# A mixture-of-experts stage on one core: routing and experts in one pass over batches of tiles

## What is computed

```python
def _L1_ffn_ref(x, router_w, router_b, expert_w, expert_b):
    router_probs = jax.nn.softmax(x @ router_w + router_b, axis=-1)
    top_p, top_i = jax.lax.top_k(router_probs, K)              # K = 2 of 8 experts
    top_p = top_p / jnp.sum(top_p, axis=-1, keepdims=True)
    expert_out = jnp.einsum('bnd,edc->bnec', x, expert_w) + expert_b
    gathered = jnp.take_along_axis(expert_out, top_i[..., None], axis=2)
    return jnp.einsum('bnk,bnkc->bnc', top_p, gathered)
...
t = t + _L1_ffn_ref(_ln_t(t), ...)                             # _ln_t: (t - mean) / sqrt(var + eps)
```

## Time and profile before

| | |
|---|---|
| median of three runs | 2795.91 us (2795.01 to 2797.33) |
| profiled execution | 2797.76 us |
| its span in the profile | 2795.8 us |
| TensorE busy | 2291.9 us, 82% |
| VectorE | 2198.8 us, 79% |
| ScalarE | 1640.6 us, 59% |
| GpSimd | 578.9 us, 21% |
| TensorE's granted clock, mean | 0.87 |

### The profile page before, as it was taken

One profiled execution on the slowest core, in us unless ns is written; L12 is line 12 of the kernel. 1 busy time (PEld: TensorE's weight loads), 2 busy tenths in 40 slices (PEclk: granted clock), 3 DMA queues, 4 the chain that ended last, 5 costly groups with the idle time before them and its releaser, 6 DMA issues. The chain is left out here.

```text
span 2795.8 us, 34597 instructions
## 1 busy us (share of the span) xinstructions
PE 2291.9 (82%) x10800; PEld 1298.5 (46%) x10800; DVE 2198.8 (79%) x3516; ACT 1640.6 (59%) x2225; POOL 578.9 (21%) x468
## 2 busy tenths in 40 slices
PE   0684646759760699999999999999999999768887
PEld 0681213747630344444444444444444444654554
DVE  5327889756598778888888888888888888668998
ACT  0113012632227478888888888888888888213665
POOL 0002340002106401210122012210200000004888
PEclk9996866555565799999999999999999999559999
DMA  4600212000004000000000000000000000000111
GB/s 148 222 19 1 120 44 78 0 9 1 1 1 121 5 1 1 1 1 1 1 1 1 1 1 1 1 1 1 1 1 1 1 1 1 9 0 16 34 34 38
DMA packets 81398, 63.93 MB, mean 23 GB/s; under 512 B 11745, under 2 KB 79329, under 8 KB 79729
## 3 DMA queue, kind: packets, MB, share of 16 engines
q1 hardware_dynamic: 74000, 60.28, 6.7%
q10 hardware_dynamic: 7264, 1.94, 0.3%
HBM read 36.97 MB, written 25.17 MB: 22 GB/s over the span
## 5 line engine op out<-in xcount | busy, mean ns | idle before, releaser
L1753 ACT ACTIVATE inner<-banks,key_bias,scales 128x1024 f32<-128x1024 f32 x512 | 617.3, 1206 | 211.0 <-PE banks L1626 205.8
L1875 DVE TENSOR_TENSOR weights_low<-weights,weights_high 128x1024 f16<-128x1024 f32 x512 | 675.5, 1319 | 17.1
L1760 ACT ACTIVATE weights<-inner 128x1024 f32<-128x1024 f32 x512 | 541.1, 1057 | 16.1 <-DVE weights_low L1875 0.3
L1871 DVE CAST weights_high<-weights 128x1024 f16<-128x1024 f32 x512 | 371.1, 725 | 180.7 <-ACT weights L1760 168.1
L1626 PE MATMUL banks<-queries_high,keys_high 128*128 128x512 f16 x1024 | 304.6, 379 | 0.7 <-ACT inner L1753 0.7
L1641 PE MATMUL banks<-weights_high,tokens_low 128*128 128x512 f16 x1024 | 304.6, 379 | 0.0
L1626 PE MATMUL banks<-queries_low,keys_high 128*128 128x512 f16 x1024 | 304.6, 379 | 0.0
L1641 PE MATMUL banks<-weights_low,tokens_high 128*128 128x512 f16 x1024 | 304.6, 379 | 0.0
L1626 PE MATMUL banks<-queries_high,keys_low 128*128 128x512 f16 x1024 | 304.6, 379 | 0.0
L1641 PE MATMUL banks<-weights_high,tokens_high 128*128 128x512 f16 x1024 | 304.5, 379 | 0.0
L1949 POOL CAST sums_high<-sums 128x512 f16<-128x512 f32 x32 | 39.4, 1230 | 1089.8 <-ACT sums L1743 1071.8
(11 more groups left out here) (432 smaller groups left out, 3751.3 us busy)
## 6 DMA issues: line engine op xcount, KB each, us to landing
images_a<-in_x SPq DMA_DIRECT2D x4, 2048.0 KB, 16.6
tokens_scratch<-images_a SPq DMA_DIRECT2D x4, 2048.0 KB, 13.1
images_b<-tokens_scratch SPq DMA_DIRECT2D x32, 256.0 KB, 2.8
mixed_scratch<-images_a SPq DMA_DIRECT2D x4, 2048.0 KB, 13.1
spare<-in_x SPq DMA_DIRECT2D x32, 256.0 KB, 2.9
result<-group_result SPq DMA_DIRECT2D x32, 256.0 KB, 2.3
images_b<-mixed_scratch SPq DMA_DIRECT2D x10, 768.0 KB, 5.3
table<-tables ACTq DMA_DIRECT2D x1, 805.5 KB, 14.3
```

What stands on the lines that cost most here:

```text
L1753: act.activation(m.inner[:, t % 2, :], m.pair[t % 2], ACT.Exp, scale=m.fs[:, 1:2], bias=m.kb[:, c // QN % 2, k:k + 1]).then_inc(s.inner, 1)
L1760: act.activation(m.wt[:, t % 2, :], m.inner[:, t % 2, :], ACT.Exp).then_inc(s.outer, 1)
L1871: vec.tensor_copy(m.wH[:, t % DEEP, :], m.wt[:, t % 2, :]).then_inc(s.high, 1)
L1875: vec.tensor_tensor(m.wL[:, t % DEEP, :], m.wt[:, t % 2, :], m.wH[:, t % DEEP, :], ALU.subtract)\
```

## The change

The two stages become one, `stage_ffn`.

- The token vectors are reflected so that the direction of all ones falls on the last coordinate. A centred vector has zero there. That row of the transposed tokens is set to 1.0 (`m.ln[..., D - 1:D]`, once), and the same row of the weights holds the biases. The weights are multiplied by the reflection (`m.house`) on TensorE at the start. Reflecting a token costs a changed mean (`TILT`); normalising is then `scale * x + bias` on ScalarE.
- Router weights are eight more columns beside the experts'. Logits are made by three `F32R` matmuls of 8 columns for each tile, from the same high and low parts as the experts'.
- The work is one pass over batches of 4, 8, 8, 8 and 4 groups. While the experts of one batch run, the next batch is normalised, turned, split and routed (`prep`, in a batch's first tiles), and its ranks and gates come in seven pieces in the batch's last eight tiles (`pieces`, `exps`). Sixteen groups fit in the ring of high and low parts (`RING`).
- VectorE adds experts 0 to 3 to the image by one multiply-add each, `u = bank * gate + acc`. The order is (n, 0), (n-1, 2), (n, 1), (n-1, 3), so that no multiply-add stands right behind the one it needs. GpSimd adds the four scaled by ScalarE (256, then 128 elements), and then `u`, in three instructions per tile.
- Banks 2, 3 and 7 hold VectorE's halves, 4 and 5 ScalarE's, 0 and 1 the transposes, 6 the logits. The expert matmuls of a tile are the same six. The loops are unrolled in full.

```diff
-            lambda: stage_router(nc, held, m, ins),
-            lambda: stage_experts(nc, held, m, out),
+            lambda: stage_ffn(nc, held, m, ins, out),
...
+BATCHES = [4, 8, 8, 8, 4]
+RING = 16
+SETTLE = 11
+def batch_plan():
+    first = [sum(BATCHES[:k]) for k in range(len(BATCHES))]
+    prep, pieces, exps = {}, {}, {}
+    for k in range(1, len(BATCHES)):
+        at, slots = first[k - 1] * GRP, BATCHES[k - 1] * GRP
+        for i in range(BATCHES[k]):
+            prep.setdefault(at + i * (slots - SETTLE) // BATCHES[k], []).append(first[k] + i)
+        for i in range(7):
+            pieces[at + slots - 8 + i] = k
+        exps[at + slots - 6] = k
...
+            def expert(n):
+                t, j = divmod(n, GRP)
+                pe.wait_ge(s.low, t + 1)
+                for h, bank in ((0, m.ps[DBANK[n % 3]]), (1, m.ps[ABANK[n % 2]])):
+                    if h == 0 and n >= 3:
+                        pe.wait_ge(s.chain, place[n - 3, 3] + 1)
+                    if h == 1 and n >= 2:
+                        pe.wait_ge(s.scaled, n - 1)
...
+            pe.wait_ge(s.loaded, 32)
+            for i in range(2):
+                pe.matmul(m.pair[1][:, 512 * i:512 * i + 512], m.house, m.w8[:, 512 * i:512 * i + 512], start=True, stop=True)
+            pe.matmul(m.pair[2][:, 0:EXPERTS], m.house, m.w8[:, EXPERTS * D:], start=True, stop=True).then_inc(s.weights, 1)
+            for t in range(BATCHES[0]):
+                turn(t)
+                if t >= 1:
+                    logit(t - 1)
+            logit(BATCHES[0] - 1)
+            for n in range(NI):
+                expert(n)
+                for t in prep.get(n - 2, []):
+                    logit(t)
+                for t in prep.get(n, []):
+                    turn(t)
...
+                    e = act.activation(m.ln[:, t % 2, j, 0:D - 1], m.b[:, img, 0:D - 1], ACT.Identity,
+                                       scale=m.fac[:, 1, img:img + 1], bias=m.fac[:, 2, img:img + 1])
...
+            for n in range(NI):
+                for t in prep.get(n, []):
+                    normed(t)
+                scaled(n)
+                for t in prep.get(n - 1, []):
+                    high(t)
+                if n in exps:
+                    exps_of(exps[n])
...
+                vec.scalar_tensor_tensor(out=m.u[:, n % 4, :], in0=m.ps[DBANK[n % 3]][:, e * D:e * D + D],
+                                         scalar=m.gate[:, n, e:e + 1], in1=acc, op0=ALU.mult, op1=ALU.add)\
+                    .then_inc(s.chain, 1)
...
+                add(n, 0)
+                add(n - 1, 2)
+                add(n, 1)
+                add(n - 1, 3)
+                for t in prep.get(n - 1, []):
+                    low(t)
...
+                    pool.tensor_tensor(m.half[:, n % 2], m.pb[:, n % 3, 0:2], m.pb[:, n % 3, 2:4], ALU.add).then_inc(s.halved, 1)
...
+                    pool.tensor_tensor(m.one[:, v % 2], m.half[:, v % 2, 0], m.half[:, v % 2, 1], ALU.add).then_inc(s.paired, 1)
...
+                    pool.tensor_tensor(m.y[:, g % 2, j, :], m.one[:, v % 2], m.u[:, v % 4, :], ALU.add).then_inc(s.result, 1)
```

More of the change, by code:

```diff
@@ L1979, in _, with stage_ffn, logits @@
                         .then_inc(row[c % 2], 16)
-def stage_router(nc, held, m, ins):
-    s = semaphores(nc, held, "router", "loaded cleared v factor rooted normed turned copied stored logits shifted exp "
-                   "high low gates gates_turned gates_copied biased added")
-    SIDE = P // EXPERTS
+BATCHES = [4, 8, 8, 8, 4]
[11 more added lines that the diff above has]
+        exps[at + slots - 6] = k
+    return first, prep, pieces, exps
+def stage_ffn(nc, held, m, ins, out):
+    s = semaphores(nc, held, "ffn", "loaded cleared biased v factor rooted weights ones normed turned high low logits shifted exp gates "
+                   "tile_d tile_a chain scaled halved paired result stored0 stored1")
+    out_img = out.rearrange("b t h w -> h (b t) w")
+    stored = [s.stored0, s.stored1]
+    first, prep, pieces, exps = batch_plan()
+    LAST = NI + 2
+    batch_of = [k for k, n in enumerate(BATCHES) for _ in range(n)]
+    DBANK, ABANK = [2, 3, 7], [4, 5]
+    order = []
+    for n in range(NI + 1):
+        order += [(n, 0), (n - 1, 2), (n, 1), (n - 1, 3)]
+    order = [(n, e) for n, e in order if 0 <= n < NI]
+    place = {key: i for i, key in enumerate(order)}
+    def logits(k):
+        return m.ps[6][:, k % 2 * 256:k % 2 * 256 + BATCHES[k] * GRP * EXPERTS].rearrange("p (t e) -> p t e", e=EXPERTS)
     with nc.Block() as block:
@@ L2108, in stage_experts @@
[L2108 to L2126 removed]
+                sp.dma_start(m.bias[D - 1:D, 0:EXPERTS * D].rearrange("p (e c) -> p e c", e=EXPERTS),
+                             ins['L1_ffn_expert_b'].unsqueeze(0)).then_inc(s.biased, 16)
@@ L2131, in _, with turn, logit @@
         def _(pe):
-            def step(t, u):
+            def turn(t):
+                pe.wait_ge(s.normed, t + 1)
+                reached(pe, s.low, t - 1)
+                for j in range(GRP):
+                    mm = pe.transpose(m.ps[t % 2][:, j * P:j * P + P], m.ln[:, t % 2, j, :], m.ident)
+                mm.then_inc(s.turned, 1)
+            def logit(t):
+                k = batch_of[t]
                 pe.wait_ge(s.low, t + 1)
+                pe.wait_ge(s.weights, 2)
+                reached(pe, s.gates, k - 1)
```

357 lines of the change are left out of this document (154 added, 203 removed).

## The result

| | before | changed |
|---|---|---|
| median of the runs | 2796.62 us (2795.01 to 2797.57, 4 runs) | 2772.80 us (2768.08 to 2775.01, 4 runs) |
| profiled execution | 2797.76 us | 2768.08 us |
| its span | 2795.8 us | 2766.2 us |
| TensorE's mean granted clock | 0.870 | 0.874 |

The ratio is 0.9913, with a 95% interval of 0.9896 to 0.9930: the change is faster by 0.9%, 24 us where 79 were forecast, and outside the range given. The sign was right and the size was not. The profiled execution is the fastest of the four, so what follows explains about 30 us.

The account below looks back on a forecast made before the run. VectorE was taken to bound the expert loop, GpSimd close behind. Begin 2394.6, start-up 35.0, batch 0 53, batches 1 and 2 144, batch 3 60.1, batch 4 25.6, end 4.4: 2716.7, forecast 2717 us, range 2682 to 2765.

Parts of the forecast that it names:

- Start-up: From the stage's begin to the end of the first gates, four groups prepared at the lower clock: 35.0 us.
- Prices: Costs taken per operation in the new loop, such as six expert matmuls 1.38 us and GpSimd 1.6 us per tile.
- The port term of 4 us: In a batch's last 8 tiles, GpSimd and two-SBUF-input rank operations delay each other: 4 us added, between 0 and 10.
- The preparing stretches: Tiles during which the next batch is prepared: 51.6 us in batches 1 and 2, 43.3 in batch 3.
- Two queues nearly equal and not in step: 3 us more: Batches 1 and 2, preparing: TensorE 43.8 and ScalarE 41.8 us, with 3 us of friction giving 46.8.
- the lockstep rival: A group's three costly slots each waited out, about 6.9 us per 2.6 tiles: 2742; chance 0.28 together with longer adds.
- the preparation is planned 2 slots ahead: Expert loop: the argument given against costly TensorE and ScalarE slots each being waited out, which would give 2742.
- The clock ... 1.0 from batch 1 on: Sign to look for: TensorE's clock at 0.5 until the first gates' end, 1.0 from batch 1 on.
- The rival in which the clock stays low: TensorE stays at its lower clock throughout the loop, 457 us from 2421.6: 2883, 3% slower; chance 0.04.
- Batch 0: 16 tiles, with 8 groups prepared in the first 5: 28 us, then 4.8 and 20.4, together 53 us.
- Batch 3: Batch that prepares 4 groups: 38.5 us with friction, 4.8, then ranks 16.8, together 60.1 us.
- The multiply-adds' exclusion: VectorE multiply-adds cannot run beside GpSimd adds, 2.81 us per tile: end at 2831, 1.3% slower; chance 0.05.

Follow-up runs that it names:

- e8: The change with GpSimd's first two adds of a tile cut to 8 elements and the third adding image and `u`: 2749.07 us, ratio 0.9839.
- e2: The change with ScalarE making a group's high part before the four scaled copies of the same slot: 2735.28 us, ratio 0.9787.
- e3: The change with 8 unused filler matmuls of 256 columns before each group's router matmuls: 2759.51 us, ratio 0.9870.
- e5: e2 with each group's router matmuls also issued one tile later: 2743.70 us, ratio 0.9811.
- e6: e2 with batches of 6, 8, 8, 8 and 2 groups: 2722.84 us, ratio 0.9738.
- e10: e6 with the ranks in eight pieces from one tile earlier: 2723.30 us, ratio 0.9740.
- e9: The kernel before with only the experts' loop rewritten (multiply-adds, three GpSimd adds, banks, unrolled, high part ahead of scaled copies): 2772.45 us, ratio 0.9919.
- e12: e9 with the low part computed from one tile, as half the transposed tokens: 2773.15 us, ratio 0.9920.
- e11: e2 with four even batches of 8 groups: 2716.59 us, ratio 0.9715.

## Why the prediction was wrong

- **Start-up**, 35.0 forecast, 33.8 measured: right, with its two matmuls at the lower clock.
- **Prices.** Router matmuls 0.11 us apart at the upper clock, experts 0.23, high part 0.60, low part 0.69, multiply-adds 341 to 349 ns and three in 0.86, GpSimd 1.53 per tile (1.6 taken): all within a few per cent. (The line through the earlier trace rows gives 0.66 us for 256 elements and not 0.69; measured are 0.72.) That an fp32 record's spacing at the lower clock, halved, gives that of a rounded one at the upper held here.
- **The port term of 4 us** in the ranks: right in size, by e8. By the windows the stretches of batches 1 to 3 took 20.1, 20.9 and 17.5 us (20.4, 20.4 and 16.8).
- **The preparing stretches** are the step that failed: "Two queues nearly equal and not in step: 3 us more". That sum took the queues as full and priced no dependency between them. The wait measured there is 18.6 us in front of L2054, and the lengthening 11.0, 15.1 and 16.2 us in batches 1 to 3, part of it the clock's. The reason named against the lockstep rival, "the preparation is planned 2 slots ahead", is where it went wrong: two slots separate transposes and router matmuls in TensorE's queue, but ScalarE's high part stood behind the copies of the tile in between, and these wait for that tile's matmuls. So only one slot of 1.38 us was left to cover 2.43, as worked out above, and one to cover the 2.78 of copies and normalising. Both queues were in the order rows; the chain across them was not followed. e2 shows it: with that one order changed, the forecast's own figures appear, 51.6, 20.3, 51.7 and 20.4 us.
- **"The clock ... 1.0 from batch 1 on"** failed: 11 falls and 41 us at 0.50 after batch 0. The rival in which the clock stays low was weighed as all or nothing. What happened lies between, and follows for the most part from the wait: ten of the 11 falls came after it, and e3 and e2 raise the clock in two different ways, by filling the gap and by removing it.
- **Batch 0**, 53 forecast, 61.0 measured: 28 us were taken for its first five tiles as between 20 and 38, and the clock was 0.77 over the batch, with 27 us at 0.50. The ranks are right, 20.1 us, so the 8 us are in the preparing stretch, 40.9 where 28 and 4.8 were summed. There TensorE stands idle for 6.4 us at once, as shown above: the same chain from ScalarE's queue, longer because two groups share a slot. In e2 the batch takes 57.4 us and this idle time is still 5.4.
- **Batch 3**: in e2, without the wait before L2054 and at clock 1.00, its first part still takes 49.1 us where 43.3 was summed. TensorE has 43.9 us of work in it, 3.4 more than the forecast's 40.5 (36.4 and three tiles), and 5.2 are idle. Of these, 4.1 are the three waits for normalising shown under e2 and 1.2 one wait for a bank.
- **Rivals.** Lockstep was right in kind: the change is a case of it, with a larger price (2742 was worked out, with banks as the cause). Its sum held the very slot, copies and normalising at 2.78 us, whose part beyond 1.38 TensorE waits out in batch 3. The multiply-adds' exclusion is excluded by e8, and the clock staying low did not occur as a whole.
- **The range.** Its bounds follow from no sum that is shown: the terms named, 8, 16 and 9 down and 10, 24 and 25 up, add up to 2684 and 2776.

## What to carry to other kernels

When a change merges two stages into one pass, follow one unit of work across all queues and ask of each hand-over which instruction stands ahead of it and what that one waits for; full queues with equal sums say nothing of it. What others wait for goes ahead of what only fills, and a wait of a microsecond ahead of short matmuls can cost twice: after ten of the 18 here the clock fell. Moving an instruction also takes away what it covered, as e5 shows. VectorE operations that use two SBUF inputs or a fast mode are best kept out of a loop in which GpSimd is the busiest engine.

## What was not expected of the hardware

- **A VectorE operation can wait out a whole row of GpSimd's.** In e2_high_first a subtraction of 128 elements ahead of the ranks, 0.29 us where nothing meets it, took 4.00. VectorE and GpSimd there:

```profile
2676.97 4.00 DVE L2156 TENSOR_TENSOR exponentials<-logits,gate_sums 128x128 f32<-128x128 f32 x1
...
2680.37 0.45 POOL L2240 TENSOR_TENSOR scaled_sum<-scaled_halves 128x128 f32<-128x128 f32 x1
2683.34 0.46 POOL L2248 TENSOR_TENSOR group_result<-scaled_sum,residual_and_scaled 128x128 f32<-128x128 f32 x1 [2.52 <-DVE residual_and_scaled L2186]
```

It ended 0.15 us after GpSimd's add of 2680.37, when that engine ran out of work because it waits for VectorE's multiply-adds. The same subtraction took 3.99 us in e3 and 4.06 in e6 and e10; the low part took 3.62 and 5.07 in e9, and 4.79 or 4.80 three times in e12. In most cases the two alternate, and the cost is 0.25 us as in the earlier trace rows (e9's low part has 0.94 us in the median, 0.68 at least); the forecast's range had the price of meeting once, not of a row. No operation of this kind was longer than 0.9 us among the ranks of e11.
- **The clock falls in a loop whose TensorE is busy for 87%.** Idle times of 1.0 us followed by twelve 8-column matmuls stood ahead of ten of the 11 falls after batch 0, but eight more such places had none. The fall shown cost 6.5 us at 0.50, the eleven 3.7 on average. Idle times in front of expert matmuls went both ways too: 3.2 us in batch 1 (2550.9 to 2554.1) stood in windows at 1.00, and after 3.2 us in batch 2 (2638.2 to 2641.4) the clock was 0.51 from 2641 to 2642. What tells the two apart is not shown here.
